# A third probability buffer and value products one head pair later, in a four-layer kernel on one core

## The reference

```python
q, k, v = (qkv[:, :, 0], qkv[:, :, 1], qkv[:, :, 2])          # heads to the front
scores = jnp.einsum('bhqd,bhkd->bhqk', q, k) * scale
scores = jnp.where(causal, scores, -jnp.inf)                  # L3 only
attn = jax.nn.softmax(scores, axis=-1)
o = jnp.einsum('bhqk,bhkd->bhqd', attn, v)
x = x + gate_msa[:, None, :] * (o @ w_proj + b_proj)
```

## Time and profile before

| | us |
|---|---|
| median of 3 runs | 468.91 |
| the 3 runs | 467.64, 468.91, 472.15 |
| the profiled execution's own time | 467.21 |
| its span | 465.5 |
| TensorE busy in the span | 303.7 |
| VectorE busy in the span | 308.1 |
| ScalarE busy in the span | 240.9 |

### The profile page before, as it was taken

One profiled execution on the slowest core, in us unless ns is written; L12 is line 12 of the kernel. 1 busy time (PEld: TensorE's weight loads), 2 busy tenths in 40 slices (PEclk: granted clock), 3 DMA queues, 4 the chain that ended last, 5 costly groups with the idle time before them and its releaser, 6 DMA issues.

```text
span 465.5 us, 5838 instructions
## 1 busy us (share of the span) xinstructions
PE 303.7 (65%) x1953; PEld 148.0 (32%) x1954; DVE 308.1 (66%) x791; ACT 240.9 (52%) x422; POOL 133.6 (29%) x237
## 2 busy tenths in 40 slices
PE   0013863532065636788888888787677899899686
PEld 0002722421023522112222222464343444344264
DVE  0678787777867767978888872334477868866330
ACT  3267835663365323166666678534243356765642
POOL 0112111251344330433223004117430244444510
PEclk9999985555555577589999999999797699999899
DMA  7950062000000043100000000000017100000001
GB/s 243 418 234 0 1 137 46 0 0 0 1 1 1 0 135 90 49 1 3 1 3 2 3 2 1 0 1 0 0 38 203 34 5 4 3 3 5 2 0 45
DMA packets 12139, 19.96 MB, mean 43 GB/s; under 512 B 2599, under 2 KB 11051, under 8 KB 11435
## 3 DMA queue, kind: packets, MB, share of 16 engines
q1 hardware_dynamic: 12108, 19.59, 13.4%
HBM read 12.51 MB, written 0.52 MB: 28 GB/s over the span
## 4 chain that ended last, share of the span: by engine, by line
PE 40%; DVE 30%; ACT 11%; POOL 7%; issue 7%; SPq 2%; DMA 2%; DVEq 0%; ACTq 0%; POOLq 0%
DVE nm L960 11%; PE ps L1482 9%; PE ps L1468 5%; PE pe L1394 4%; PE ps L1535 4%; PE pe L1504 4%; POOL rstd L343 2%; PE ps L1441 2%; ACT scr L1078 2%; DVE st L538 2%; SPq L323 1%; PE ps L1265 1%; DMA big<-in_wa 1%; PE pe L1231 1%; ACT junk L1070 1%
## 5 line engine op out<-in xcount | busy, mean ns | idle before, releaser
L960 DVE TENSOR_REDUCE nm<-ps 128x1 f32<-128x512 f32 (+2 forms) x224 | 131.9, 646 | 28.7 <-PE ps L1468 27.7
L1191 ACT ACTIVATE scr<-pe 128x1024 f32<-128x1024 f32 (+3 forms) x128 | 107.4, 867 | 74.7 <-PE pe L1504 73.9
L1468 PE MATMUL ps<-big 64*128 64x512 bf16 (+3 forms) x256 | 71.0, 378 | 11.5 <-DVE nm L960 11.5
L1482 PE MATMUL ps<-scr 128*32 128x512 f32 (+3 forms) x512 | 59.7, 538 | 9.0 <-ACT scr L1166 7.5
L343 POOL TENSOR_TENSOR rstd<-var,half 128x4 f32<-128x4 f32 x26 | 28.5, 1097 | 102.6 <-DVE var L543 77.1
L1504 PE MATMUL pe<-big 64*128 64x512 bf16 (+3 forms) x256 | 49.7, 358 | 2.2 <-ACT scr L1191 1.6
L449 POOL TENSOR_SCALAR_AFFINE_SELECT scr<-scr 128x256 f32<-128x256 f32 x64 | 25.7, 407 | 37.5 <-ACT scr L1191 36.2
L1468 PEld LDWEIGHTS ps<-big 64*128 64x128 bf16 x256 | 20.7, 100 | 38.6 <-DVE nm L960 33.0
L437 POOL CAST nm<-nm 128x16 bf16<-128x16 f32 x16 | 3.1, 196 | 97.0 <-DVE nm L960 97.0
L1504 PEld LDWEIGHTS pe<-big 64*128 64x128 bf16 x256 | 13.5, 94 | 52.4 <-ACT scr L1191 31.6
L548 DVE TENSOR_SCALAR xn<-x_tok,mv,rstd 128x128 f32<-128x128 f32 x60 | 17.1, 347 | 15.8 <-POOL rstd L343 15.8
(11 more groups left out here) (222 smaller groups left out, 584.7 us busy)
## 6 DMA issues: line engine op xcount, KB each, us to landing
big<-tern SPq DMA_DIRECT2D x48, 128.0 KB, 2.4
big<-in_wa SPq DMA_DIRECT2D x1, 2304.0 KB, 12.4
w<-in_w SPq DMA_DIRECT2D x2, 1152.0 KB, 19.2
big<-in_wa SPq DMA_DIRECT2D x1, 1344.0 KB, 6.1
big<-in_w SPq DMA_DIRECT2D x1, 1024.0 KB, 14.3
w<-in_w SPq DMA_DIRECT2D x1, 896.0 KB, 19.9
rowg<-in_rowg SPq DMA_DIRECT2D x1, 832.0 KB, 18.2
row<-in_row SPq DMA_DIRECT2D x1, 640.0 KB, 14.4
```

Source lines behind the costliest of these rows:

```text
L960: v.tensor_reduce(dst, src[:, 0:w * len(hs)].rearrange("p (h w) -> p h w", w=w), AX.X, ALU.max, negate=True).then_inc(sem(f"a{a}_max"), 1)
L1191: s_.activation(P[:, kt % 2, 2 * p:2 * p + 2, q0:S], E[(e - 1) % 2][:, :, q0:S], ACT.Exp, scale=SCALE).then_inc(sem(f"a{a}_p"), 1)
L1468: last = t_.matmul(dst[:, k * wd:(k + 1) * wd], stack_of(a, 0, b, HG * g + h, qt * 128, (qt + 1) * 128), stack_of(a, 1, b, HG * g + h, 0, ...
L1482: last = t_.matmul(bank[6][32 * h:32 * h + 32, q0:S], V[b][:, kt, HG * g + h, :], P[:, kt % 2, h, q0:S], start=(kt == 0), stop=(kt == TB - 1),
```

## The change

`P` gets a third buffer. Its memory is that of `qT` and `hqT`, which become views of one tensor `ints_` with the same size as one buffer. Buffers are taken by the running number of the key tile modulo 3 on ScalarE, GpSimd and TensorE. An exponential may now run three tiles ahead of the value products instead of two. The value products move from the odd steps to the even ones, one head pair later: tile 0 of a unit goes from the end of step 3 to the end of step 4, tile 1 to step 6, tile 2 to step 0 and tile 3 to step 2 of the next unit, each behind the ring items of its step. The last two tiles are multiplied after the loop.

```diff
-        qT = sb("qT", [128, 3, B, S], BF16)
+        ints_ = sb("ints", [128, 8 * 512], BF16)
+        qT = ints_[:, 0:3 * B * S].rearrange("p (m b t) -> p m b t", m=3, b=B)
-        hqT = sb("hqT", [128, 2, 512], BF16)
+        hqT = ints_[:, 3 * B * S:].rearrange("p (i t) -> p i t", i=2)
-        P = scr[:, 0:2 * HG * S].rearrange("p (i h t) -> p i h t", i=2, h=HG)
+        P = [scr[:, i * HG * S:(i + 1) * HG * S].rearrange("p (h t) -> p h t", h=HG) for i in range(2)]
+        P += [ints_[:, :].bitcast(F32).rearrange("p (h t) -> p h t", h=HG)]
...
-                        block_ = P[:, kt % 2, 2 * p:2 * p + 2, 128 * kt:128 * kt + 128]
+                        block_ = P[s // 2 % 3][:, 2 * p:2 * p + 2, 128 * kt:128 * kt + 128]
...
-                                if TB * u + kt >= 2:
-                                    act.wait_ge(sem(f"a{a}_pv"), TB * u + kt - 1)
-                                s_.activation(P[:, kt % 2, 2 * p:2 * p + 2, q0:S], E[(e - 1) % 2][:, :, q0:S], ACT.Exp,
+                                if TB * u + kt >= 3:
+                                    act.wait_ge(sem(f"a{a}_pv"), TB * u + kt - 2)
+                                s_.activation(P[(TB * u + kt) % 3][:, 2 * p:2 * p + 2, q0:S], E[(e - 1) % 2][:, :, q0:S], ACT.Exp,
...
-                                             P[:, kt % 2, h, q0:S], start=(kt == 0), stop=(kt == TB - 1),
+                                             P[(TB * u + kt) % 3][:, h, q0:S], start=(kt == 0), stop=(kt == TB - 1),
...
-                        if p == 1 and s > 1:
-                            probs_out((s - 2) // 8, (s - 2) // 2 % 4)
+                        if p == 0 and s >= 4:
+                            probs_out((s - 4) // 8, (s - 4) // 2 % 4)
+                    probs_out(7, TB - 2)
                     probs_out(7, TB - 1)
```

## The result

The changed kernel takes 489.92 us (median of 4 runs, 484.96 to 490.76) against 468.54 before: the ratio is 1.042, with a 95% interval of 1.0371 to 1.0469. The forecast had the sign, slower by 7.1 us; the measured loss is 21.4 us, three times that, and outside the range. The profiled execution took 489.53 us with a span of 487.8, so 22.3 more than the one of before in both. The lines of the changed kernel are two further down: L1484 holds the value products, L1438 parts, L1470 the maxima, L1506 the scores, L1193 the exponentials. In the rows PE is TensorE, PEld its weight loads, DVE VectorE, ACT ScalarE and POOL GpSimd.

The account below looks back on a forecast made before the run. It took a TensorE-VectorE loop through three ring banks, plus a longer GpSimd chain once a unit, as the bound. 467.2 + 2.8 (full attention) + 4.3 (causal) = 474.3, 476.0 us against the median; range 469 to 482.

Parts of the forecast that it names:

- The third buffer is worth nothing by itself: Exponentials on ScalarE wait for scores alone, so a third buffer frees nobody and only makes the later order legal: 0.
- Value products moved behind parts, +0.71 and +0.69 a unit: TensorE stands about 1.5 us at parts: full-attention unit 12.37 to 13.08 us, causal unit 9.23 to 9.92.
- the sum: Whole kernel: 467.2 + 2.8 (full attention) + 4.3 (causal) = 474.3 us, 476.0 against the median; TensorE's clock at 1.00.
- The copy's wait, counted at its full 0.30 and 0.61 only inside the replay: Value products' wait for the previous unit's output copy, 0.30 us a full-attention unit, 0.61 causal, 7.5 in all, goes.
- the replay: Step-by-step timing of one unit in the new order from rows of the old trace: 13.08 us full attention, 9.92 causal.
- the faster rival: All 7.5 us of the copy's wait come back and nothing takes its place: 459.7, about 461 us; chance 7%.
- a longer chain: Once a unit: last maximum on VectorE, four GpSimd operations, then parts on TensorE; 1.34 us full attention, 1.27 causal.
- The clock: Rival: TensorE's clock falls in the wait before parts, in up to 11 units, 6 to 14 us on top; chance 9%.
- The rival's price per fall (0.9 + 0.4): Clock rival: each fall costs 0.9 us on value products and about 0.4 more.
- The rival's 482 to 490: Time in us for the whole kernel if the clock falls in the wait before parts; chance 9%.

Follow-up runs that it names:

- two fillers: Changed kernel plus two thrown-away products of 128x512 on TensorE ahead of the wait for parts, units 1 to 6 of both layers: 476.91 us, ratio 1.0158.
- pv_first: Changed kernel with the value products of an even step right behind its scores, ahead of its ring items: 468.14 us, ratio 0.9963 to the kernel before.
- parts_late: Changed kernel with parts one maximum later (LAG 3 for 2), in step 5 behind tile 0's value products: 462.18 us, ratio 0.9831 to the kernel before.
- copy_early: Kernel before, with the copy of the previous unit's output one exponential earlier on ScalarE: 466.68 us, ratio 0.9931.
- The slowed kernels: Kernel before with three or six more copies on GpSimd ahead of its split of the maxima: 479.91 us, ratio 1.0213, and 497.46 us, ratio 1.0609.
- the estimate for two buffers: Made for a run with value products in even steps and parts one maximum later, on two buffers, expected 475 to 490 us: 474.48 us, ratio 1.01.

## Why the prediction was wrong

*The third buffer is worth nothing by itself:* right, 1.0001. In the later order it is needed; the forecast called it only what makes that order legal, which leaves out this worth.

*Value products moved behind parts, +0.71 and +0.69 a unit:* right where the clock holds. 13.11 against 13.08 and 9.80 against 9.92 in the changed kernel, and with two fillers the whole kernel is 7.3 us over the one before, where the sum had 7.1. That the totals are so close is in part luck: between the profiled executions of these two kernels the difference is 9.7, full attention takes about 4.3 more where the sum had 2.8, and the causal layer 2.9 in its units and 1.9 behind its last parts where it had 4.3 and nothing. The mechanism, that GpSimd's answer leaves TensorE nothing to do, is shown from both sides: pv_first puts the value products back ahead of parts and parts_late puts parts behind them, and either takes all of the loss away; parts_late moves parts alone. (The 398.23 in the prediction is simply the end of the run of the earlier trace rows, 393.18 and 5.05, and not "9.23 after" it; the 1.27 worked out from it is right.)

*The copy's wait, counted at its full 0.30 and 0.61 only inside the replay:* right in direction; copy_early gives back 3.2 us of the 7.5, so the faster rival was far off and the rest of its price lies beside a longer chain, as the forecast had it.

*The clock:* **this is the step that failed.** The sum took a granted clock of 1.00 and gave the fall a chance of 9%, since the waits of before left it at 1.00. It fell in 8 of the 11 units with the new wait. Against the units with two fillers, one by one, the changed kernel's are longer by 1.15, 1.43 and 1.27 in three of full attention, and by 1.52, 2.91, 1.53, 3.08 and 1.45 in five of the causal layer; the others agree within 0.2. That is 14.3 us in the profiled execution, on top of the order's 7. (The two profiled executions differ by 12.6 in all, since with two fillers the end of the causal layer takes 2.5 longer; the clock fell there.) The rival's price per fall (0.9 + 0.4) fits the six falls where TensorE stays at the low clock for about 3.5 us, in either layer. In the two causal units where it stays there for nearly 7 us the price is double, 2.91 and 3.08. The rival's 482 to 490 held the time; its chance was wrong.

The Trainium skill (TensorE: Matmul & The Clock Gate, section "A second HAM failure mode: psum-queue depth-cycling") says that TensorE's short idle times between groups of matmuls can make the clock swing. The changed kernel's trace agrees: 0.50 for about 3.5 us, twice for nearly 7, behind waits of 1.48 and 1.31. The slowed kernels speak against taking it as a rule for every wait: 1.55 and 2.33 us in full attention passed at 1.00.

What stays open is what in the stretch around a wait decides. In the changed order 1.48 us lowered the clock in some units and not in others of one execution, in the old order 2.33 did not, and in the causal layer of the same run 1.9 to 2.05 did, and 1.76 once in three times. Length alone is ruled out. The order of the work around the wait is not enough either: the units of full attention in the changed kernel have the same order and the same wait, and two keep the clock where three lose it. No run here tells what else decides, or why two of the falls last twice as long.

## What to carry to other kernels

Before work is moved later in an in-order queue, look at what it was covering: here the value products filled the time of another engine's answer, and the wait that the change removed was mostly beside that longer one. When a move opens a new wait on TensorE, price it twice, once at the clock of before and once with the clock down behind it, and give the second its own weight even if waits half as long have been harmless in the kernel before (0.77 here). A replay from a few rows of the timeline was good to 0.12 us a unit for the changed kernel at the full clock and to 0.22 for the variant that wins; the estimate for two buffers, 0.5 for a pair of steps, was far off. Once a replay shows which item stands idle, move that item, not its neighbour.

## What the runs showed of the hardware that was not expected

Two products of 0.60 us together, whose result is thrown away, made a kernel 2.6% faster: with them TensorE waits 0.21 and 0.57 us in place of 1.48 in a unit of full attention, and its clock stays at 1.00 in every unit but the first, which starts at the low clock. A wait of 2.33 us in one order left the clock at 1.00 in all five units that have it, while 1.31 in another was followed by a fall to 0.50 that cost up to 3.1 us. And the same wait in the same order of work, within one execution, lowered the clock in some units and not in others.
